# Scores of two heads at a time, each on half of TensorE's rows, in a layer kernel of attention and experts

## The reference

```python
xn = _layernorm(x)
# attention: 16 heads of 8 channels
qkv = (xn @ Wqkv + bqkv) ...            # q, k get a rotary embedding
scores = einsum('bhtd,bhsd->bhts', q, k) / sqrt(8)
attn = softmax(scores) @ v              # then @ Wout + bout
# experts: 16 experts of width 64, the two best per token, and a shared one
g = sigmoid(xn @ gate_w + gate_b); values, idx = top_k(g, 2); values /= sum(values)
mlp(x, wg, wu, wd) = (silu(x @ wg) * (x @ wu)) @ wd
out = x + attn_out + xn + mlp_shared(xn) + sum(values * mlp_expert(xn)[idx])
```

## Time and profile before

| | us |
|---|---|
| median of 3 runs (242.8 to 243.15) | 243.12 |
| the profiled execution | 242.69 |
| its span in the trace | 240.0 |
| PE busy | 216.0 (90%) |
| DVE busy | 168.7 (70%) |
| POOL busy | 161.2 (67%) |
| ACT busy | 137.1 (57%) |

### The profile page before, as it was taken

How to read it: one execution, slowest core, us unless ns; L and a number is a source line. 1 busy time by engine, 2 the same in 40 slices (tenths; PEclk the granted TensorE clock), 3 DMA queues, 4 the chain that set the end, 5 groups by cost and what they waited for, 6 DMA issues and landing times.

```text
span 240.0 us, 4717 instructions
## 1 busy us (share of the span) xinstructions
PE 216.0 (90%) x1576; PEld 134.1 (56%) x1576; DVE 168.7 (70%) x374; ACT 137.1 (57%) x257; POOL 161.2 (67%) x236
## 2 busy tenths in 40 slices
PE   0485698898989999989999999999999999999993
PEld 0354454464655666666756656666756656675552
DVE  5997869999585766998656768976666666655221
ACT  2455111155568665656566665667575866667662
POOL 9186763789847259888848295999893855637802
PEclk9997789999999999999999999999999999999999
DMA  6925354620527240502662414116516450211101
GB/s 231 358 66 152 104 163 131 189 92 2 182 71 219 80 145 5 153 0 75 204 202 60 159 46 126 30 54 175 150 31 190 142 155 17 76 50 43 47 0 44
DMA packets 35952, 26.51 MB, mean 110 GB/s; under 512 B 4236, under 2 KB 30156, under 8 KB 35916
## 3 DMA queue, kind: packets, MB, share of 16 engines
q1 hardware_dynamic: 35292, 25.33, 34.9%
q10 hardware_dynamic: 636, 0.88, 1.0%
HBM read 18.53 MB, written 7.47 MB: 108 GB/s over the span
## 4 chain that ended last, share of the span: by engine, by line
PE 74%; DVE 11%; DMA 5%; SPq 4%; issue 2%; ACT 2%; POOL 1%; DVEq 0%; ACTq 0%; POOLq 0%
PE PV L548 12%; PE Y L581 12%; PE S2b L529 7%; PE S2a L529 6%; PE S1a L508 5%; PE S1b L508 5%; PE FB L386 3%; PE FB L387 3%; PE FB L388 3%; PE FA L387 3%; PE FA L386 3%; PE FA L388 3%; DMA x_sb<-in_x 2%; DVE mx L1000 2%; PE FA L441 2%
## 5 line engine op out<-in xcount | busy, mean ns | idle before, releaser
L1000 DVE TENSOR_REDUCE mx<-S1a 128x2 f32<-128x512 f32 x65 | 44.6, 686 | 17.3 <-PE S1a L508 17.3
L1000 DVE TENSOR_REDUCE mx<-S1b 128x2 f32<-128x512 f32 x63 | 43.2, 685 | 19.2 <-PE S1b L508 19.0
L734 ACT ACTIVATE probs<-S2b 128x512 f32<-128x512 f32 x62 | 37.1, 598 | 29.5 <-PE S2b L529 29.5
L734 ACT ACTIVATE probs<-S2a 128x512 f32<-128x512 f32 x62 | 37.1, 599 | 17.2 <-PE S2a L529 14.6
L1114 POOL TENSOR_TENSOR gu<-gu,gate 128x512 f32<-128x512 f32 (+1 forms) x30 | 38.2, 1274 | 9.1 <-DVE gu L988 7.6
L581 PE MATMUL Y<-gu,wd_sb 128*128 128x512 f32 (+1 forms) x72 | 37.3, 599 | 0.3 <-POOL gu L1101 0.3
L746 ACT ACTIVATE th<-FA 128x512 f32<-128x512 f32 (+1 forms) x36 | 21.5, 597 | 25.3 <-PE FA L388 25.1
L548 PE MATMUL PV<-probs,vx 128*32 128x256 f32 x512 | 35.1, 384 | 0.2 <-ACT probs L734 0.2
L1112 POOL TENSOR_TENSOR gate<-gate,wbc 128x512 f32<-128x512 f32 x27 | 34.5, 1279 | 0.7 <-DMA wbc<-route_w 0.6
L508 PE MATMUL S1a<-k_hat,q_hat 96*128 96x256 bf16 x130 | 25.2, 275 | 1.5 <-DVE mx L1000 1.5
L508 PE MATMUL S1b<-k_hat,q_hat 96*128 96x256 bf16 x126 | 24.3, 274 | 1.6 <-DVE mx L1000 1.4
(11 more groups left out here) (163 smaller groups left out, 408.4 us busy)
## 6 DMA issues: line engine op xcount, KB each, us to landing
wbc<-route_w SPq DMA_DIRECT2D x64, 128.0 KB, 3.0
q_hat<-q_parts SPq DMA_DIRECT2D x32, 96.0 KB, 2.6
k_hat<-k_parts SPq DMA_DIRECT2D x32, 96.0 KB, 2.6
k_parts<-parts SPq DMA_DIRECT2D x8, 192.0 KB, 2.1
q_parts<-parts SPq DMA_DIRECT2D x8, 192.0 KB, 2.2
x_sb<-in_x SPq DMA_DIRECT2D x4, 256.0 KB, 3.9
q_parts<-parts SPq DMA_DIRECT2D x8, 128.0 KB, 2.1
k_parts<-parts SPq DMA_DIRECT2D x8, 128.0 KB, 2.1
```

The costliest lines, as they stand in the source:

```text
L734: nc.scalar.activation(probs[:, head % (2 * NQ), :], exp_bank(head)[:], ACT.Exp, scale=SCALE).then_inc(exp_done, 1)
L1000: nc.vector.tensor_reduce(mx[:, (q // QB) % 2, (q // 2) % 2, :, q % 2, i], S1[use % 2][:].rearrange("p (t s) -> p t s", t=SB), axis=AX.X, ...
```

## The change

The two heads of a pair of rows move apart: rows 0 to 47 and 64 to 111 (`HROWS = 64`), each followed by three maxima rows of its own (to row 50 and 114). `k_hat` has one copy and no zeros, so the two memsets of it go. A score matmul names only its head's 48 or 51 rows and so stands on one half of the array's rows. `max_pair` and `exp_pair` take two heads that lie in different halves, in the order head A, head B, head A, head B, into the two banks at once; both banks have to be free before the first of the four. Quad q's head i lies in half (q + i) % 2. The block begins with the gate products; the two pairs come at steps 0 and 2, `attend` at step 1, and at step 2, ahead of the second pair, the early fillings, the down product, `maxima_to_rows` (now of the even block itself) and the late fillings. ACT copies the gate after the first two exponentials. `kones` comes by four small DMAs instead of two, the maxima rows of a half by two instead of one.

```diff
+HROWS = 64
+KALL = KROWS + PARTS
...
+def score_row_half(q, i):
+
+    return (q + i) % 2
...
-        k_hat = sb("k_hat", [P, 2, H // 2, 2, T], bf16)
+        k_hat = sb("k_hat", [P, 2, H // 2, T], bf16)
...
-            def max_scores(q, i):
...
-                bank = take_s(("max", q * NQ + i))
-                for t in range(SB):
-                    last = nc.tensor.matmul(bank[:, t * T:(t + 1) * T], q_hat[0:MROW, slot, pair, t * P:(t + 1) * P],
-                                            k_hat[0:MROW, slot, pair, r, :], start=True, stop=True)
-                last.then_inc(s1_ready, 1)
+            def max_pair(q, first):
...
+                banks = [take_s(("max", q * NQ + i)) for i in (first, first + 1)]
                 for t in range(SB):
+                    for i, bank in zip((first, first + 1), banks):
+                        pair, rows = NQ * hg + i, HROWS * score_row_half(q, i)
+                        last = nc.tensor.matmul(bank[:, t * T:(t + 1) * T],
+                                                q_hat[rows:rows + KROWS, slot, pair, t * P:(t + 1) * P],
+                                                k_hat[rows:rows + KROWS, slot, pair, :], start=True, stop=True)
+                        if t == SB - 1:
+                            last.then_inc(s1_ready, 1)
...
                 for s in range(SB):
+                    for i in (first, first + 1):
+                        pair, rows = NQ * hg + i, HROWS * score_row_half(q, i)
+                        last = nc.tensor.matmul(exp_bank(q * NQ + i)[:, s * T:(s + 1) * T],
+                                                k_hat[rows:rows + KALL, slot, pair, s * P:(s + 1) * P],
+                                                q_hat[rows:rows + KALL, slot, pair, :], start=True, stop=True)
...
                 for i in range(NQ):
+                    if i == 0 and n < NCHUNKS:
+                        up(n, "hg")
                     if i == 1 and 0 <= blk - 1 < NBLK:
                         attend(blk - 1)
                     if i == 2:
                         for kind, g in early_b(blk):
                             fill_b(kind, g)
-                    if i == 3 and 0 <= n - 2 < NCHUNKS:
-                        down(n - 2)
-                    if i == 3:
+                        if 0 <= n - 2 < NCHUNKS:
+                            down(n - 2)
+                        if negated_half(blk) is not None:
+                            maxima_to_rows(negated_half(blk))
                         for kind, g in late_a(blk):
                             fill_a(kind, g)
-                    if 0 <= blk < FOUR_BANKS:
-                        exp_scores(blk, i)
-                    if 0 <= q < NBLK:
-                        max_scores(q, i)
-                    if i == 0 and n < NCHUNKS:
-                        up(n, "hg")
+                    if i % 2 == 0 and 0 <= blk < FOUR_BANKS:
+                        exp_pair(blk, i)
+                    if i % 2 == 0 and 0 <= q < NBLK:
+                        max_pair(q, i)
...
-            nc.vector.memset(k_hat[0:MROW, 0].rearrange("p a r t -> p (a r t)").bitcast(u32), 0).then_inc(hat_zeroed, 1)
...
+                    if i == 2 and negated_half(blk) is not None:
+                        maxima_to_rows(negated_half(blk))
-                    if i == 3:
+                    if i == 2:
                         for kind, g in late_a(blk):
                             read_a(kind, g)
```

More of the change, by code:

```diff
@@ L129, in bank_uses @@
                 s["max", q * NQ + i] = len(s)
-            if i == 0 and transposed_half(blk) is not None:
-                s["M", transposed_half(blk)] = len(s)
+            if i == 1 and negated_half(blk) is not None:
+                s["M", negated_half(blk)] = len(s)
     return a, b, s
@@ L297, in _ @@
             for s in range(2):
-                sp.dma_start(k_hat[MROW:KALL, s], kones).then_inc(ld_kones, 16)
+                for r in range(2):
+                    sp.dma_start(k_hat[HROWS * r + KROWS:HROWS * r + KALL, s], kones).then_inc(ld_kones, 16)
             sp.dma_start(wout_sb[:], wout).then_inc(ld_wout, 16)
@@ L335, in load_max @@
                 half = h % 2
-                sp.dma_start(q_hat[MROW:KALL, (h // 2) % 2, NQ * half:NQ * (half + 1), :],
-                             mT[0:MROWS * NQ, h % 2, :]).then_inc(max_ld[h % 4], 16)
+                for r in range(2):
+                    sp.dma_start(q_hat[HROWS * r + KROWS:HROWS * r + KALL, (h // 2) % 2, NQ * half:NQ * (half + 1), :],
+                                 mT[PARTS * NQ * r:PARTS * NQ * (r + 1), h % 2, :]).then_inc(max_ld[h % 4], 16)
             def load_route(g, c):
@@ L643, in _ @@
                             spare_rope(2 * (n - 1) + half)
-                    if i == 0 and transposed_half(blk) is not None:
-                        maxima_to_rows(transposed_half(blk))
                     if i == 3 and n < NCHUNKS:
@@ L735, in exponentials, with gate_tanh, gate_copy @@
                                      scale=SCALE).then_inc(exp_done, 1)
+            def gate_tanh(n):
+                rows = I if n % NCH == 0 else P
+                act.wait_ge(fa_ready, A_USE["hg", n] + 1)
+                if n >= 2:
+                    act.wait_ge(fb_read, B_USE["hu", n - 2] + 1)
+                nc.scalar.activation(th[0:rows, n % 2, :], FA[0:rows, :], ACT.Tanh, scale=0.5).then_inc(th_ready, 1)
+            def gate_copy(n):
+                rows = I if n % NCH == 0 else P
+                if n - 2 >= GATES_COPIED:
+                    act.wait_ge(gu_weighted, n - 1)
+                nc.scalar.activation(gate[0:rows, n % 2, :], FA[0:rows, :], ACT.Copy,
+                                     scale=0.5 if n % NCH == 0 else 1.0).then_inc(fa_read, 1)
             for blk in range(FIRST, LAST + 1):
@@ L1180 @@
     cos, sin = rope_tables()
-    kones = np.zeros((MROWS, H // 2, 2, T), np.float32)
-    for r in range(2):
-        kones[PARTS * r:PARTS * (r + 1), :, r] = 1.0
+    kones = np.ones((PARTS, H // 2, T), np.float32)
     bf = mybir.dt.np(mybir.dt.bfloat16)
```

74 lines of the change are left out of this document (27 added, 47 removed).

## The result

| | before | after |
|---|---|---|
| median of 10 runs | 243.14 us (242.24 to 244.51) | 246.17 us (244.41 to 248.77) |
| ratio | | 1.0106, 95% interval 1.0077 to 1.0135 |
| profiled execution, span | 242.69, 240.0 | 245.4, 243.6 |
| first gate product of block 3 | 66.63 us | 72.98 us |
| the same of block 29 | 221.29 us | 224.63 us |

Forecast were 237.0 us and a range up to 245.0.

The account below looks back on a forecast made before the run. TensorE was taken to bound the steady part, with VectorE as full in the start. The terms -22.95 + 10.5 + 4.1 + 1.5 + 1.7 - 0.5 gave -5.65 us, so 237.0 us; range 230.5 to 245.0.

Parts of the forecast that it names:

- term 5: Start: PE's saving is worth nothing since VectorE is as full; uncovered VectorE time costs +1.7 us, bounds 0 and 6.7.
- terms 1 to 4: Steady part: score overlap -22.95, shape changes +10.5, both banks at once +4.1, transposed maxima +1.5 us.
- term 6: End: 24 exponential matmuls, 1.35 us of PE, in a partly busy stretch save 0.5 us, bounds 0 and -1.3.
- Terms 1 and 2: Steady part's scores: two heads run together, -22.95 us; more changes of the array's shape, +10.5 us.
- rival 3: Score pairs: weights of both halves load one after the other, +7.8 us, 250.5; chance 0.14 together with no overlap.
- the lock: Maxima pairs take both S1 banks at once, so PE can't fill one while VectorE reads the other; +4.1 us, steady part.
- term 4: Transposes moved to the even block: PE waits for GpSimd 0.5 us in block 8, +1.5 in all, bounds 0 and 4.
- Term 3: Steady part, both maxima banks taken at once: VectorE overruns eight blocks, +4.1 us, bounds 0.5 to 5.9.
- the overrun: VectorE's work exceeding the shortened block where the routing runs: 1.3 us in block 8, 1.15 in block 16, 4.1 in sum.
- 3 and 4: Score pairs: weights of the halves load in turn, 250.5 us, or halves don't overlap, 256.4; chance 0.14 together.
- Rival 1: Around the score pairs, shape changes are cheap or hide behind weight loads; 232 us, chance 0.16.
- Rival 2: Lock of two banks dominates: PE's first pair waits for maxima in most blocks; 243.0 us, equal to before, chance 0.16.

Follow-up runs that it names:

- m_next_block: Changed kernel with the transposes of the maxima behind attend of the next block, for all halves; 243.42 us, ratio 0.9964 to before.
- halves_old_order: Kernel before's order, head by head, in the layout of halves, all scores of a block on one half so none overlap; 268.36 us, ratio 1.1019 to before.
- halves_old_cross: Like halves_old_order, but a step's exponential and maximum heads lie in opposite halves, issued in turn, so they can overlap; 244.28 us, ratio 1.0048 to before.
- m_next_block_start: Changed kernel with the transposes of the first three halves (blocks -2, 0, 2) behind attend of the next block; 242.48 us, ratio 0.9960 to before.
- m_after_attend: Changed kernel with the transposes directly behind attend in the same block, their copy behind its second maximum; 248.09 us, ratio 1.0200 to before.
- crossed_next_but8: crossed_pairs with the transposes of block 8 alone back in block 8; 236.87 us, ratio 0.9703 to before.
- crossed_only: Changed kernel with only the crossing: one head's exponential score beside another's maxima score; median 246.62 us, four runs from 243.93 to 248.8, no ratio given.
- the first two experiments: halves_old_order and halves_old_cross: kernel before's order in the layout of halves, without and with overlap; 268.36 and 244.28 us.
- crossed_pairs: m_next_block, but each matmul pair is one head's exponential score beside another's maxima score, where a block has both; 238.54 us, ratio 0.9784 to before.

## Why the prediction was wrong

Forecast was a sum of -5.65 us; the span grew by 3.6. Of the 9.25 us between them 4.65 lie in the start (term 5), 3.85 in the steady part (terms 1 to 4 and what they leave out) and 0.76 in the end (term 6). The step that failed is in the main one: the transposes' move was priced as one wait in block 8 and two like it. What it does to the start, and what it costs in every even block, was put at nothing.

**Terms 1 and 2 held.** Block 22 of m_next_block has, like block 22 before, neither transposes nor a wait and is 0.46 us shorter, where 0.90 - 0.405 = 0.495 was forecast. The pairs' overlap and the changes of shape are confirmed together, in size and place. That the overlap comes to half of 45.9 us was taken over from column strips, and halves_old_order and halves_old_cross bear it out.

"TensorEngine Tiling (Array Packing)" of the Trainium skill, section "Tiling Modes", has tiles of a mode load and multiply in parallel and a change of the mode drain the array. The traces agree with the first: two loads of 94 to 98 ns each go at once, and pairs follow at 0.11 us. Of the second they show that a change costs 0.08 to 0.19 us, not that it is a drain. The rule on loads that stood beside rival 3 ("TensorE: Matmul & The Clock Gate" of the Trainium skill, section "LDWEIGHTS (loading the stationary operand)") doesn't bound a pair here, since its two loads go at once.

**Term 5, the start, was mis-sized: 1.7 us (bound 6.7) against 6.35 (6.7 by the blocks' own starts).** It counted the lock in half of the blocks. It didn't count that the transposes' move puts PE behind GpSimd in block -2, where GpSimd still makes the low parts of q and k. The term 4 argument, made for block 8, was never applied to the start; there the wait is 2.26 us, the copy and the pair come behind it, and block -2 is 3.9 us longer. m_next_block_start gave 3.7 of it back. Block -3 begins 1.2 us late already: PE is busy for 7.00 of 7.00 us from 29 to 36 us in both kernels, with a granted clock of 0.80 before and 0.56 now, near the lower level of 1.2 GHz. It was 0.50 to 0.59 in all kernels here but three (0.80 to 0.83: before, m_after_attend, m_next_block_start). The last two have the changed kernel's instructions up to there, with scores on half rows, so the same program gets either clock. What sets it is not settled. Block -2 is 3.9 of the 6.35 us, the late begin of block -3 is 1.2, and the other 1.2 lie in blocks -3, -1 and 0 to 2.

**What the steady sum left out: the transposes have a price of their own.** "They move up ... to the even one" was priced as a wait for GpSimd (term 4, 1.5 us) and nothing else. Measured are, by the even blocks of m_next_block (block 24 apart), 0.54 us in the mean for each of 13 halves, 7.0 us. In block 22 it is 0.21 for the two transposes with the changes of shape around them (some 0.11 of it, an estimate, is their own work: they have 128 columns each, and a score of 256 takes 0.1125) and 0.38 because their copy holds one of two banks that the next pair needs. Before, they stood between products and `attend`, where a change was due anyway, and cost 0.07 us, 0.9 in 13 blocks. "One copy, moved" was in my order listing of VectorE, and I asked what the copy waits for, not who waits for its bank. Terms 1 and 2 in the steady part make -12.45; with 7.0 more and 0.9 less it is -6.35, and -3.0 was measured. That leaves 3.35 for terms 3 and 4, where 5.6 stood. The split is rough, since the 0.54 holds some of their waits.

**Term 4 was 0.1 us in the changed kernel, where 1.5 stood.** In block 8 PE waited 0.10 us for GpSimd at the transposes, in no other steady block longer than that. The mechanism is real: 2.26 us in block -2, 0.57 in block 8 of crossed_next_but8, 4.0 in m_after_attend. But in block 8 of the changed kernel PE reaches the transposes 15.1 us after the gate products of block 6, not 14.4. Other waits grew in the steady part: those of over 0.15 us that are not for the copy rose from 2.0 to 4.2 us, 1.0 of it in block 17, where a filling waits for VectorE to free bank FB.

**Term 3 was inside its bounds and wrong in its sum with the rest.** Where the copy is out of the way the lock costs 2.85 us in the steady part; 4.1 was forecast for it there (bounds 0.5 and 5.9). That the whole run differs by 4.2 is not that forecast come true, since 1.0 of it is the start. The place was off as well: the overrun comes in block 9, behind the routing's block 8, and part of it is for ScalarE's banks, which the term left out. In the changed kernel the lock costs about 0.5 us of the steady part (crossed_only), and the reading is that the copy holds a bank at the same place. Two waits that end at one point don't add. Blocks 8 and 16 took 7.14 and 7.06 us, "not below 6.8" as said.

**Term 6, the end, had -0.5 us and came to +0.26.** At 229.94 and 233.47 PE waits for ScalarE's exponentials, 0.37 and 0.36 us, where before it did not wait for them. A pair needs two of those banks at once, which would explain it, but no run tested the end apart.

**The rivals.** 3 and 4 fell by the first two experiments. Rival 1 fell: the changes cost the 0.08 to 0.19 us that the rows before had shown. Rival 2 had the nearest total (243.0), but it put the waits at the first pair of a block and for a maximum; six of them are at the second pair and for the copy. What was not tried apart: the maxima rows of a half by two DMAs instead of one, and the gate's copy behind two exponentials.

## What to carry to other kernels

Packing two small matmuls on halves of the array pays best if they come in few, long runs: count the changes of shape of every instruction that is moved beside them, small transposes too. When an instruction moves, ask three things of it: is its input made by then in every block, the first ones included; what shape stands on both sides; and whose bank does its reader hold meanwhile. And let the two matmuls of a pair end in banks with different readers, so that a pair waits for one reader of each kind and not for one reader twice.

## What the runs showed that was not expected

- A float32 product right behind scores on half rows takes 0.33 us to its successor instead of 0.235, beside the 0.10 ahead of it (140.34, 140.66, 140.99 above). Before, such a product takes 0.32 as well, but it starts 0.08 us before the scores are over (177.91, 178.05, 178.37), so nothing is lost. From the last two scores to the second product it is 0.65 us against 0.46.
- The largest differences between these kernels in the steady part lie in two blocks, 9 and 17: they take 5.22 to 9.54 us, by where VectorE stands when the transposes or the next scores come. m_next_block's runs spread from 240.28 to 245.66 us, those of crossed_pairs from 238.28 to 238.92.
